# Edge-run starts by comparison products, two queues for the first edges, and layer one's end with four sum buffers

## The reference, cut to what matters

```python
edge_index = jnp.stack([src, dst])
x = _layernorm(x + L0(x, src, dst))               # 10 hops, 0.9 * normalised aggregate + 0.1 * h0
x = _layernorm(x + L1(x, edge_index, edge_attr))  # one hop with edge attributes, two dense layers, batch norm
x = _layernorm(x + L2(x, src, dst))               # 2 hops, out = h @ W.T + b + x @ Wr.T + br
x = _layernorm(x + L3(x, edge_index))             # attention over edges, 4 heads, mean over the heads
# L1: h = (segment_sum(x[src] + edge_attr @ We + be, dst) + x) @ W1 + b1
#     out = relu(batchnorm(h)) @ W2 + b2
# L3: logits = leaky_relu(a_src[src] + a_dst[dst]); alpha = softmax over the edges of a dst (with self loops)
```

## Time and profile before

| | |
|---|---|
| median of 3 runs | 1274.06 us |
| profiled execution | 1275.39 us, its span 1273.5 us |
| granted TensorE clock, mean | 0.893 |
| busy | TensorE 1156.5 us (91%), VectorE 873.9 (69%), ScalarE 631.0 (50%), GpSimd 62.7 (5%) |
| first use of loaded edges | 36.64 us |
| hop 11 begins, ends its first 300 products | 717.46 us, 736.57 us |
| first masked product of layer three | 826.43 us |

### The profile page before, as it was taken

The page is one execution under the profiler, slowest core; times in us unless marked ns, Lnnn a source line. Parts: engine busy times, 40 slices in busy tenths (PEclk is TensorE's granted clock), DMA queues, the critical chain, the costliest instruction groups (busy, mean ns, idle before and its releaser), DMA issues.

```text
span 1273.5 us, 40137 instructions
## 1 busy us (share of the span) xinstructions
PE 1156.5 (91%) x16724; PEld 1078.6 (85%) x16724; DVE 873.9 (69%) x2375; ACT 631.0 (50%) x1161; POOL 62.7 (5%) x113
## 2 busy tenths in 40 slices
PE   0588889888999999999999899499999999999996
PEld 0588888888999999999963799389989998998996
DVE  1899999996434443434551534689888988888887
ACT  0576776761000000000012402478898898888986
POOL 2000000000111111111000011000000000000000
PEclk9865555567999999999999699699999999999999
DMA  1544444430000000000000000000000000000000
GB/s 27 85 66 67 65 68 71 63 60 11 3 3 2 3 3 2 3 3 3 3 2 1 1 3 2 2 2 2 3 2 2 2 2 2 2 2 2 7 12 13
DMA packets 133768, 21.42 MB, mean 17 GB/s; under 512 B 133041, under 2 KB 133458, under 8 KB 133618
## 3 DMA queue, kind: packets, MB, share of 16 engines
q1 hardware_dynamic: 132190, 18.75, 9.8%
q10 hardware_dynamic: 1332, 0.33, 0.1%
q0 software_dynamic: 96, 0.16, 0.0%
HBM read 18.43 MB, written 0.80 MB: 15 GB/s over the span
## 4 chain that ended last, share of the span: by engine, by line
PE 69%; DVE 21%; issue 5%; ACT 3%; DMA 1%; SPq 1%; POOL 0%; DVEq 0%; ACTq 0%; POOLq 0%
PE bank L1795 31%; PE bank L1915 18%; PE bank L1911 9%; DVE ohk L998 7%; DVE ohp L1000 4%; PE bank L1740 3%; DVE raw L988 2%; PE bank L1732 1%; DVE Mr L1512 1%; PE bank L1977 1%; ACT Mr L909 1%; PE bank L1651 1%; PE bank L1906 1%; PE bank L1765 1%; DVE oht L958 1%
## 5 line engine op out<-in xcount | busy, mean ns | idle before, releaser
L1795 PE MATMUL bank<-GH,C 128*128 128x128 f16 x7100 | 397.9, 219 | 0.0
L1795 PEld LDWEIGHTS bank<-GH,C 128*128 128x128 f16 x7100 | 396.9, 98 | 0.1
L1915 PE MATMUL bank<-F,Mr 128*128 128x260 f16 (+1 forms) x2520 | 343.3, 268 | 6.3 <-DVE Mr L1512 4.7
L1915 PEld LDWEIGHTS bank<-F,Mr 128*128 128x128 f16 x2520 | 219.1, 98 | 30.2 <-DVE Mr L1512 5.6
L1512 DVE TENSOR_TENSOR Mr<-Mr,C 128x640 f16<-128x640 f16 x433 | 196.5, 486 | 47.1 <-ACT Mr L909 45.8
L754 ACT ACTIVATE plo<-bank 128x256 f32<-128x256 f32 (+1 forms) x84 | 30.1, 360 | 363.2 <-PE bank L1795 346.7
L1911 PE MATMUL bank<-FN,C 128*128 128x130 f16 x2260 | 209.8, 220 | 0.0
L1157 DVE TENSOR_TENSOR S<-bank,plo 128x256 f32<-128x256 f32 (+1 forms) x84 | 33.1, 394 | 211.5 <-ACT plo L754 211.4
L909 ACT ACTIVATE Mr<-eaT 128x640 f16<-128x640 f32 x218 | 164.9, 822 | 16.9 <-PE bank L1915 16.0
L1911 PEld LDWEIGHTS bank<-FN,C 128*128 128x128 f16 x2260 | 164.2, 98 | 9.5 <-DVE r L1420 0.5
L909 ACT ACTIVATE Mr<-cold,eaT 128x640 f16<-128x640 f32 x215 | 162.7, 824 | 19.2 <-PE bank L1915 18.3
(11 more groups left out here) (253 smaller groups left out, 1019.4 us busy)
## 6 DMA issues: line engine op xcount, KB each, us to landing
raw<-in_edges_dram SPq DMA_DIRECT2D x242, 68.0 KB, 2.1
xs<-in_x_dram SPq DMA_DIRECT2D x1, 800.0 KB, 4.4
out_dram<-xs SPq DMA_DIRECT2D x4, 160.0 KB
cold<-in_L_gnn_W_dram ACTq DMA_DIRECT2D x2, 64.0 KB
z<-in_L_gnn_att_src_dram SPq DMA_DIRECT2D x1, 128.0 KB, 2.7
z<-in_L_gnn_att_dst_dram SPq DMA_DIRECT2D x1, 128.0 KB, 3.1
out_dram<-xs SPq DMA_DIRECT2D x1, 128.0 KB
wts<-in_L_gnn_W_dram ACTq DMA_DIRECT2D x4, 16.0 KB
```

Of the source, the lines that this page charges most:

```text
L1795: last = pe.matmul(bank[:, b, jj * 2 * D:(jj + 1) * 2 * D], C[:, t, (t0 + jj) * P:(t0 + jj + 1) * P], GH[:, par, t, :], start=t == 0 and j ...
L1915: return pe.matmul(bank[:, k, a_:z_], Mr[:, mi % RB, j * P:(j + 1) * P], F[:, t, a_:z_], start=start, stop=t == T - 1)
```

## The change

1. The search. `dst` is loaded whole into 125 partitions of 5 rows of 160 and the row before (476 KB in 124 rows of 3840 bytes, and the first row apart). VectorE takes the difference of each row with the one before (`jump`, 125x800 f32) and compares the 256 bounds with each row's first element (`less`). TensorE's products of `less` with `jump` (f32, 5 for each half of the bounds, 161 columns) give for each bound the row in which it falls, and 160 times the row's number in a last column. VectorE counts in it. Two products with the identity turn row number and count into one row of 128 starts, and VectorE writes it as integers. The gather and the way through DRAM are gone.
2. The edge loads of group 0: SyncE issues windows 0 to 5, ScalarE's queue windows 6 to 10.
3. Layer one's end: sums in four buffers (`sum2`: two of `V`, two of `xc`), features behind moments and scales, and the w2 products of blocks 4 to 6 inside hop 11's arriving products (`AHEAD = 4`).
4. Into layer three: L1846 waits for GpSimd's copy alone (`s_zx`); the diagonal's addition is cut by blocks; scores of 4 blocks, `nad` and `xw` of the first head, their copy, the first `Vx` and F's first high part are moved ahead of the flag, into other banks.

```diff
-    R = E // ROW
+    RP = 125
+    RC = E // (ROW * RP)
...
+                dsts = tb("dsts", [RP, (RC + 1) * ROW], I32)
+                jump = tb("jump", [RP, RC, ROW + 1], F32)
+                bound = tb("bound", [P, 2 * P], F32)
+                less = tb("less", [RP, RC, 2 * P], F32)
+                firsts = tb("firsts", [RP, RC], F32)
                 wlo = tb("wlo", [P, 2], F32)
-                cnt = tb("cnt", [P, 8], F32)
...
-        pas = bank[:, 7, 0:2 * H * T]
+        pas = bank[:, 0, 0:2 * H * T]
+        pnad0 = bank[:, 2:4].rearrange("p a b -> p (a b)")[:, 0:NG * P]
...
+        def sum2(b):
+
+            return (V if b % 4 < 2 else xc)[:, b % 2]
...
-            sp.dma_start(fs[0:1, 0:R].bitcast(I32), dst.rearrange("(r c) -> c r", c=ROW)[0:1, :], allow_slow_non_contiguous=True).then_inc(s_first, 16)
-            sp.wait_ge(s_start, 1)
-            sp.dma_start(starts_d.ap().rearrange("(p b) -> p b", b=2), st_i[:]).then_inc(s_startd, 16)
-            sp.wait_ge(s_startd, 16)
-            sp.dma_start(starts_row, starts_d.ap()[None, :]).then_inc(s_startrow, 16)
-            sp.wait_ge(s_startrow, 16)
+            sp.dma_start(dsts[1:RP, :], bass.AP(dst.tensor, dst.offset + (RC - 1) * ROW, [[RC * ROW, RP - 1], [1, (RC + 1) * ROW]])).then_inc(s_first, 16)
+            sp.dma_start(dsts[0:1, ROW:], dst.rearrange("(p c) -> p c", c=RC * ROW)[0:1, :]).then_inc(s_first, 16)
...
-            for g in range(2):
-                for half in range(2):
-                    load_half(g, g, half)
+            sp.wait_ge(s_startrow, 1)
+            load_half(0, 0, 0)
+            for half in range(2):
+                load_half(1, 1, half)
+            sp.wait_ge(s_startrow, 2)
...
+            pool.iota(wlo[:], pattern=[[P * W, 2]], base=0, channel_multiplier=W, allow_small_or_imprecise_dtypes=True).then_inc(s_iota, 1)
...
-            pool.wait_ge(s_rowidx, 1)
-            for b in range(2):
-                pool.indirect_dma_start(out=rows_i[:, b, :], out_offset=None, in_=dst.rearrange("(r c) -> r c", c=ROW),
-                                        in_offset=bass.IndirectOffsetOnAxis(ap=row_i[:, b:b + 1], axis=0)).then_inc(s_rows, 16)
...
                 pool.wait_ge(s_free, 12 * NB + b + 1)
                 if b >= 2:
-                    pool.wait_ge(s_y, NB + b - 1)
+                    pool.wait_ge(s_m7, b - 1)
+                pool.tensor_copy(z[:, b % 2, 0:n, D:2 * D], xs[:, t0:t0 + n, :]).then_inc(s_zx, 1)
+                if b >= 2:
                     pool.wait_ge(s_xcu, m + 1)
-                pool.tensor_copy(z[:, b % 2, 0:n, D:2 * D], xs[:, t0:t0 + n, :]).then_inc(s_g, 1)
                 pool.tensor_tensor(xc[:, b % 2, 0:n, :], xs[:, t0:t0 + n, :], biases[:, 0:1, :].to_broadcast([P, n, D]), ALU.add).then_inc(s_g, 1)
-                pool.wait_ge(s_g, 2 + 3 * b + 2)
-                pool.tensor_tensor(xc[:, b % 2, 0:n, :], xc[:, b % 2, 0:n, :], biases[:, 1:2, :].to_broadcast([P, n, D]), ALU.add).then_inc(s_g, 1)
-                pool.wait_ge(s_g, 2 + 3 * b + 3)
-                pool.sem_inc(s_xc, 1)
+                pool.wait_ge(s_g, 2 + b + 1)
+                pool.tensor_tensor(xc[:, b % 2, 0:n, :], xc[:, b % 2, 0:n, :], biases[:, 1:2, :].to_broadcast([P, n, D]), ALU.add).then_inc(s_xc, 1)
...
+            act.wait_ge(s_startrow, 1)
+            w0, w1_ = HALVES[1]
+            _, begins = nc.values_load_multi_w_load_instructions(
+                starts_row[0:1, w0:w1_], engines=[mybir.EngineType.Activation], min_val=0, max_val=E,
+                skip_runtime_bounds_check_because="the starts are counts, and were held to E on the chip, and SLOT edges to no node follow the last one")
+            for w, s in enumerate(begins):
+                act.dma_start(raw[:, 0, w0 + w], edges[bass.ds(s, SLOT), :].rearrange("(k p) c -> p k c", p=P)).then_inc(s_raw[0], 16)
...
-                    last = act.activation(xs[:, t0 + j, :], V[:, b % 2, j, :], ACT.Identity, bias=shift2(b)[:, j:j + 1], scale=inv2(b)[:, j:j + 1])
+                    last = act.activation(xs[:, t0 + j, :], sum2(b)[:, j, :], ACT.Identity, bias=shift2(b)[:, j:j + 1], scale=inv2(b)[:, j:j + 1])
...
@@ -853,21 +873,16 @@
                     high_x(b - 3)
                 if b >= 4:
                     turned(b - 4)
+                if b == 8:
+                    copy_nad(0, pnad0)
             act.activation(small[0:1, 61:62], onesP[0:1, :], ACT.Exp)
             act.wait_ge(s_arg, 1)
             act.activation(ex[:], ex[:], ACT.Exp, scale=1.0 / XS).then_inc(s_exp, 1)
+            act.activation(small[0:1, 62:63], onesP[0:1, :], ACT.Sigmoid)
+            high_f(0, 0)
             act.wait_ge(s_flag3, 1)
             dense3 = act.value_load(flag[0:1, 1:2], min_val=0, max_val=1)
...
-            c.add(v.tensor_copy(first_f, fs[0:1, 0:R].bitcast(I32)))
+            c.add(v.memset(bound[:, 0:1], 0.0))
+            c.add(v.memset(dsts[0:1, 0:ROW].bitcast(F32), 0.0))
+            c.add(v.memset(jump[:, :, ROW:ROW + 1], float(ROW)))
+            for k in range(8):
+                c.here()
+                c.add(v.tensor_scalar(bound[:, 2 ** k:2 ** (k + 1)], bound[:, 0:2 ** k], float(W * 2 ** k), None, ALU.add))
+            v.wait_ge(s_first, 32)
             c.here()
-            v.tensor_scalar(first_f, first_f, 0.0, None, ALU.add).then_inc(s_firstf, 1)
-            v.wait_ge(s_firstb, 1)
+            own_rows = dsts[:].rearrange("p (r c) -> p r c", c=ROW)
+            c.add(v.tensor_copy(firsts[:], own_rows[:, 1:, 0]))
+            v.tensor_tensor(jump[:, :, 0:ROW], own_rows[:, 1:], own_rows[:, 0:RC], ALU.subtract).then_inc(s_jump, 1)
+            c.here()
+            for k in range(RC):
+                v.tensor_scalar(less[:, k], bound[0:RP], firsts[:, k:k + 1], None, ALU.is_gt).then_inc(s_less, 1)
+            v.wait_ge(s_iota, 1)
+            for b in range(2):
+                v.wait_ge(s_rows, b + 1)
+                v.tensor_copy(cnt[:, b:b + 1], bank[:, 6 + b, ROW:ROW + 1]).then_inc(s_cnt, 1)
+                c.add(v.tensor_scalar(found[:], bank[:, 6 + b, 0:ROW], wlo[:, b:b + 1], None, ALU.is_lt, ALU.add, accum_out=cnt[:, 2 + b:3 + b]))
+                c.here()
+                v.sem_inc(s_cnt, 1)
+                v.wait_ge(s_start, b + 1)
+                v.tensor_scalar(starts_row[:, b * P:(b + 1) * P], bank[0:1, b, 0:P], -float(ROW), 0.0, ALU.add, ALU.max).then_inc(s_startrow, 1)
...
                 v.wait_ge(s_y, b + 1)
-                v.tensor_tensor(V[:, b % 2, 0:n, :], bank[:, b, 0:n * D].rearrange("p (t d) -> p t d", d=D), xs[:, t0:t0 + n, :], ALU.add).then_inc(s_free, 1)
+                if b >= 4:
+                    v.wait_ge(s_ap, b - 3)
+                v.tensor_tensor(sum2(b)[:, 0:n, :], bank[:, b, 0:n * D].rearrange("p (t d) -> p t d", d=D), xs[:, t0:t0 + n, :], ALU.add).then_inc(s_free, 1)
...
             for b in range(NB + 2):
-                if b >= 2:
-                    l1_features(b - 2)
                 if b < NB:
                     l1_moments(b)
                 if 1 <= b <= NB:
                     l1_scales(b - 1)
+                if b >= 2:
+                    l1_features(b - 2)
...
+            v.wait_ge(s_cst, 4)
+            v.memset(own16, XS ** 0.5).then_inc(s_own, 1)
...
                     v.tensor_tensor(z[:, b % 2, 0:n, 0:D], s_, cols(5, t0, n), ALU.mult).then_inc(s_o, 1)
+                    own = bass.AP(C[:].tensor, C[:].offset + t0 * (TP + P), [list(C[:].ap[0]), [TP + P, n], [1, P]])
+                    v.tensor_tensor(own, own, ident16[:, None, :].to_broadcast([P, n, P]), ALU.add).then_inc(s_self, 1)
...
+            def scaled(h, g):
+
+                gi = h * NG + g
+                t0 = g * NT
+                v.wait_ge(s_xw, gi + 1)
+                if gi >= 2:
+                    v.wait_ge(s_F, gi - 1)
+                v.tensor_tensor(Vx[gi % 2], pxw[:, :, None, :].to_broadcast([P, NT, 2, S1]),
+                                E2[:, :, h, t0:t0 + NT].rearrange("p e t -> p t e")[:, :, :, None].to_broadcast([P, NT, 2, S1]), ALU.mult).then_inc(s_vx, 1)
+
+            scaled(0, 0)
...
+            def begin(b):
+
+                pe.wait_ge(s_cnt, 2 * b + 2)
+                pe.wait_ge(s_cst, 2)
+                pe.matmul(bank[0:1, b, 0:P], cnt[:, b:b + 1], ident[:], start=True, stop=False)
+                pe.matmul(bank[0:1, b, 0:P], cnt[:, 2 + b:3 + b], ident[:], start=False, stop=True).then_inc(s_start, 1)
+
+            pe.wait_ge(s_jump, 1)
+            for b in range(2):
+                for k in range(RC):
+                    if b == 0:
+                        pe.wait_ge(s_less, k + 1)
+                    last = pe.matmul(bank[:, 6 + b, 0:ROW + 1], less[:, k, b * P:(b + 1) * P], jump[:, k, :], start=k == 0, stop=k == RC - 1)
+                    if b == 1 and k == 2:
+                        begin(0)
+                last.then_inc(s_rows, 1)
+            begin(1)
...
+            AHEAD = 4
+
+            def l1_down(b):
+
+                t0, n = BL[b]
```

(71 more changed lines are left out.)

115 lines of the change are left out of this document (30 added, 85 removed).

## The result

The changed kernel takes **1252.02 us** (median of 4 runs, 1251.6 to 1252.93), the kernel before beside it 1274.17 us (4 runs, 1273.95 to 1274.54): a ratio of 0.983, 95% interval 0.981 to 0.984. Forecast were 1255.8 us, in a range from 1247.5 to 1262. The direction came out as forecast, and parts 1 and 2 came near their forecast size; part 3 gave 2.3 us more than forecast, through a step that the prediction had wrong.

A forecast was written before the change was run, and what follows sets the result against it. Bound by round trips before the first edges, VectorE/TensorE waits at layer one's end, and the step into layer three: 11.3 + 3.9 + 3.1 = 18.3 us off the 1274.06 us median gives 1255.8 us, range 1247.5 to 1262.

The forecast's parts named there:

- Part 1: The search and group 0's edge loads: first use of the edges at 25.3 instead of 36.64 us, gain 11.3 us.
- Part 2: Layer one's end: VectorE needs 2.9 us a block instead of 4.36, w2 products interleaved with hop 11; gain 3.9 us.
- part 3: The step into layer three: work moved from behind the flag to ahead of it; gain 3.1 us, bounds 0.5 and 4.5.
- the 53-row store: Store at the output's end, 17 GB/s on about one engine; from it the 124-row first transfer was put on four.
- the two turns of the counts: In the search, two TensorE products turning row number and count into a row: 1.2 us.
- Loads: Group 0's eleven edge loads from two queues, bounded by the engines at 136 GB/s: 7.1 us, before 9.2.
- The build: Stage after the first edges that keeps VectorE full to about 290 us; time cut ahead shifts it one for one.
- rival B: Layer one's end: TensorE's clock stays at half through the interleaved blocks, gain only 0.4 us, time 1259.3 us; chance 18%.
- the scores end where they did: Ahead of the flag: moved products and copy take back the 0.65 us gained, so the scores still end at 814.4.
- the wait of 1.0 us: L1846's 1.04 us wait at 799.18 for GpSimd's two additions; now only the copy is awaited, 0.65 us of it kept.
- the branch's hole: 2.7 us of nothing before the last L1846, at the branch out of hop 12; expected to be late next.
- The bound of 4.5 us: Upper bound of the gain into layer three, if the hole at the branch out of hop 12 closes.

The follow-up runs named there:

- three shifted versions of before: The kernel before with 8, 20 and 45 instructions without effect added at the start of TensorE's program: 1273.95, 1273.93 and 1274.92 us.

## Why the prediction was right, and where it was off

**Part 1, forecast 11.3, measured 12.6 us.** The transfer was read rightly out of the 53-row store: four engines, landing forecast at 9.3, measured 8.70 (8.56 to 10.45 over the runs). From the landing to the first edge load 8.9 us were forecast and 8.3 measured; the two turns of the counts were set at 1.2 us and take 0.73 (14.80 to 15.53). Loads 7.1 and 7.1 us, which is partly luck: the prediction had the engines bound them at 136 GB/s, and windows show up to 192. The step mis-sized is the turn (0.5 us); 0.6 us is the landing, which lies within its scatter.

**The build, forecast 0.** Every group keeps its 11.39 us; the build's end came 0.75 us sooner than that (from the first key operation to it 255.59 us before, 254.84 after). It takes 254.18 to 255.60 us in ten traces of changed kernels and 254.19 to 255.63 in four of the kernel before, so the 0.75 us is the run and no part of the change. So is the 0.26 us from there to the first w2 product (408.75 against 409.01; 408.45 to 409.63 and 408.19 to 409.64 in all traces).

**Part 2, forecast 3.9, measured 3.95 us.** The clock rose at 704.6 us, 8.6 us after hop 11's first product and just before the 48 products ended (704.71); rival B, whose sign was a half clock beyond 12 us, is out. The mechanism, TensorE's waits, is the forecast one. That the sizes agree to 0.05 us is luck: the stretch of the same code has two values 1.6 us apart, and the profiled run has the longer one. The prediction had not asked what buffers, order and interleaving bring alone; the order alone gives nearly the same.

**Part 3, forecast 3.1, measured 5.4 us; the step that failed.** Behind the flag it was right: F's high part 1.54 us after the flag instead of 4.90 is 3.4 us, forecast 3.2. Ahead of the flag the prediction had "the scores end where they did": of the wait of 1.0 us it kept 0.65, because the branch's hole would stay, and had the moved products and the copy take that back. There 2.05 us were gained against the trace of before (81.52 to 79.47 us from the end of the 300 to the flag; three shifted versions of before have 80.93 to 81.32, which would make it 1.5 to 1.9). By the experiments this is 0.84 (turns that wait only for the copy), less 0.44 (the moved products), and 1.65 us that is left over: 1.15 us of the hole (1.40 less 0.25) and about 0.5 us of slower issue behind it, which the changed kernel does not have even with the old waits. The bound of 4.5 us named the hole's closing, but gave the whole stretch ahead of the flag 1.3 us; with the turns' wait gone as well, it was 2.05. So the step that failed is the one by which the hole stays and the moved work takes back the 0.65 us. That the moved products cost 0.44 us is shown, and so is what the wait gives; why the hole closed is open.

**The sum.** 12.6 + 1.0 + 3.95 + 5.4 = 22.96 us of the profiled executions, 22.2 us of the medians, against 18.3. Of the excess of 4.7 us by the traces, 2.3 is part 3, 1.3 the head (of which 0.6 the landing), 1.0 the build with what follows it up to w2. So about 1.6 of the 4.7 us is scatter and not the change.

**What is better than both.** 112 + 12 rows: 1248.3 us, 3.7 us under the changed kernel, by one more transfer. All nine runs of the two versions with 112 and 12 rows lie under 1249.6 us, all four of the changed kernel above 1251.5.

## What to carry to other kernels

Before a transfer is put on the critical path, ask how its rows divide: split off the remainder (112 + 12 for 124) so that the large part goes over all engines; here this was worth 3.7 us. When two edits remove the same wait, try each alone: here the interleaving could have been left out. Before a single trace is taken for the size of an effect, look at the same stretch in other traces of the same code: here one had two values, 1.6 us apart. And a hole that no wait explains is not to be counted as fixed: give it a chance of its own in the range.

## What the runs showed that was not expected

- **GpSimd's first iota comes later beside a long first transfer.** With the 124 rows on four engines it comes between 9.96 and 10.89 us (seven traces), with 62 + 62 rows at 10.45 us, with 112 + 12 rows at 8.44 and 8.34 us. In the 112 + 12 version:

```profile
8.44 0.14 POOL L578 IOTA wlo<- 128x2 f32 x1 [7.61 <-issue]
```

and in the changed kernel:

```profile
10.56 0.30 POOL L577 IOTA wlo<- 128x2 f32 x1 [9.72 <-issue]
```

Why is not settled; nobody waits for it in these versions, but it would bound a faster search.

- **Edge loads from two queues** (68 KB each) move up to 192 GB/s in a window of 1 us, where one queue had 124 to 136: one sequencer's issues, 0.56 us apart, come to 124.
- **The same products take 29.8 or 31.4 us** from the first w2 product to the end of the 300, with the granted clock at 0.50 for 13.7 or 17.1 us. The cause is open.
- **A landing scatters**: 8.56 to 10.45 us for the same transfer, more than several of the effects here. The build scatters by 1.4 us as well; what is steady to some hundredths is each group of it (11.39 us) and the stretches from the end of the 300 to the flag and on to the first masked product.
